# Other homes for the last expert's down weights, and an alternating order of two engines behind the last sort

## The reference

```
y = shared_mlp(x)                                   # silu(x@sg_w) * (x@su_w) @ sd_w, hidden size 1536
for i in range(16):
    gate_feature = x * pe[i] @ gate_w + gate_b
    gate_weight, gate_idx = top_k(gate_feature, 384) # sorted, per token
    u = take(x, gate_idx) * softmax(gate_weight)
    y = y + (silu(u @ eg_w[i]) * (u @ eu_w[i])) @ ed_w[i]
yn = layernorm(y) * ln_g + ln_b
out = x + silu(yn @ m1_w + m1_b) @ m2_w + m2_b
```

## Time and profile before

| | us |
|---|---|
| device time, median of 3 runs | 6455.91 |
| the runs, lowest to highest | 6451.81 to 6457.31 |
| the profiled execution, its own time | 6456.37 |
| its span in the trace | 6454.4 |

### The profile page before, as it was taken

One profiled execution on the slowest core, in us unless ns is written; L12 is line 12 of the kernel. 1 busy time (PEld: TensorE's weight loads), 2 busy tenths in 40 slices (PEclk: granted clock), 3 DMA queues, 4 the chain that ended last, 5 costly groups with the idle time before them and its releaser, 6 DMA issues. The chain is left out here.

```text
span 6454.4 us, 69413 instructions
## 1 busy us (share of the span) xinstructions
PE 5694.2 (88%) x16428; PEld 2987.6 (46%) x16428; DVE 5155.9 (80%) x6434; ACT 2631.7 (41%) x4313; POOL 4120.3 (64%) x3617
## 2 busy tenths in 40 slices
PE   8989999889888888888888888888888888889888
PEld 4545555445444444444444444444444444445554
DVE  4011012999999999999999999999999999999831
ACT  0000000445454545454545454545454545544431
POOL 0543024667777777777777777777777776768630
PEclk9999999999999999999999999999999999999999
DMA  3366245000000000000000000000000000001101
GB/s 124 111 154 163 109 122 156 23 22 15 15 15 16 15 16 15 18 14 30 1 30 1 30 2 29 15 16 15 16 16 15 16 15 16 15 30 37 37 24 45
DMA packets 113766, 254.55 MB, mean 39 GB/s; under 512 B 36104, under 2 KB 46862, under 8 KB 113322
## 3 DMA queue, kind: packets, MB, share of 16 engines
q1 hardware_dynamic: 70442, 180.18, 8.0%
q0 software_dynamic: 42880, 69.46, 4.4%
HBM read 214.75 MB, written 34.58 MB: 39 GB/s over the span
## 5 line engine op out<-in xcount | busy, mean ns | idle before, releaser
L1390 PE MATMUL mask_ps<-key,neg_ident 125*125 125x480 f32 (+7 forms) x4128 | 1886.0, 578 | 477.3 <-DVE key L1787 443.3
L1485 POOL TENSOR_TENSOR pay<-pay_side,pay 125x480 int32<-125x480 int32 (+11 forms) x1075 | 1288.7, 1199 | 643.3 <-DVE pay L1810 637.3
L1669 ACT COPY mask_ps<-key 125x960 f32<-125x960 f32 (+6 forms) x1107 | 947.9, 856 | 1587.4 <-DVE pay L1827 930.6
L1477 POOL TENSOR_TENSOR pay_side<-pay 125x480 int32<-125x480 int32 (+11 forms) x1075 | 1284.6, 1196 | 355.5 <-DVE pay L1827 209.1
L1390 PEld LDWEIGHTS mask_ps<-key,neg_ident 125*125 125x125 f32 x4128 | 732.7, 193 | 1394.7 <-DVE key L1787 882.1
L1810 DVE COPY_PREDICATED pay<-mask_ps,pay 125x960 f32<-125x960 int32 (+6 forms) x1075 | 1231.8, 1146 | 74.4 <-PE mask_ps L1390 54.4
L1777 DVE TENSOR_TENSOR key<-mask_ps,key 125x960 f32<-125x960 f32 (+6 forms) x1075 | 1082.8, 1007 | 20.9 <-PE mask_ps L1390 16.9
L1787 DVE TENSOR_TENSOR key<-mask_ps,key 125x960 f32<-125x960 f32 (+6 forms) x1075 | 1083.9, 1008 | 1.1
L1390 PE MATMUL mask_ps<-key_top,neg_ident 125*125 125x480 f32 (+3 forms) x1472 | 588.3, 527 | 150.8 <-DVE key_top L1787 139.5
L1337 PE MATMUL slot_ps<-w_exp,hid 128*125 128x384 f32 x1920 | 676.1, 491 | 10.4 <-issue 8.7
L1309 PE MATMUL slot_ps<-u_feat,w_exp 128*128 128x312 f32 (+1 forms) x2304 | 666.6, 427 | 0.7 <-ACT u_feat L1564 0.7
(11 more groups left out here) (191 smaller groups left out, 5707.7 us busy)
## 6 DMA issues: line engine op xcount, KB each, us to landing
w_rel_g<-L_gnn_W SPq DMA_DIRECT2D x16, 2304.0 KB, 23.4
w_exp<-L_ffn_ed_w SPq DMA_DIRECT2D x16, 2304.0 KB, 8.4
messages_dram<-rows_g SPq DMA_DIRECT2D x12, 1875.0 KB
w_exp<-L_ffn_eg_w SPq DMA_DIRECT2D x16, 1152.0 KB, 5.4
w_exp<-L_ffn_eu_w SPq DMA_DIRECT2D x16, 1152.0 KB, 7.9
messages_dram<-rows_g SPq DMA_DIRECT2D x20, 375.0 KB
root_w_g<-L_gnn_root SPq DMA_DIRECT2D x2, 2304.0 KB
w_exp<-L_ffn_sg_w SPq DMA_DIRECT2D x4, 1152.0 KB, 5.8
```

The lines of the kernel that those rows point to most:

```text
L1390: last = pe.matmul(mask, neg_ident[0:TP, 0:TP], operand, start=False, stop=True, skip_group_check=True)
L1477: pool.tensor_tensor(shares(pay_was(turn, u), turn, u)[1].bitcast(I32), first, second, ALU.add).then_inc(pays_added, 1)
L1485: pool.tensor_tensor(second, shares(pay_was(turn, u), turn, u)[1].bitcast(I32), first, ALU.subtract).then_inc(pays_taken, 1)
L1669: act.copy(seed_of(turn, u), compared(turn, u)[0]).then_inc(seeded, 1)
```

## The change

Three things are changed, all of them in what follows the last sort.

- The last expert's down weights get places of their own. Four of the six blocks go into `first_rows`, a view of the memory of `h_feat`; they are loaded right behind that expert's gate and up weights. Two blocks go into `w_piece_down`, loaded when the last group of `piece_out` has been filled. A new semaphore `late_loaded` counts the two transfers, and `last_out` takes the place of `expert_out` for this expert on TensorE.
- ScalarE does an exponential and a copy of `piece_out` in turn, five times; then, behind the wait for the inverted sums, a scaling and a copy in turn, five times.
- GpSimd does a `weigh` and a sum of `piece_out` in turn, five times, then the other five sums.

The numbers of operations, of matmuls and of bytes loaded stay the same; one transfer of 2304 KB becomes one of 1536 KB and one of 768 KB.

```diff
--- before.py
+++ after.py
@@ -1042,6 +1042,9 @@
         bias_rows = sb("bias_rows", [TP, D])
         w_exp = sb("w_exp", [P, KD, D])
         w_piece_down = sb("w_piece_down", [P, KK, D])
+
+        NFIRST = KD - 2
+        first_rows = h_feat[:, :, :].rearrange("p k c -> p (k c)")[:, 0:NFIRST * D].rearrange("p (k n) -> p k n", n=D)
         key = sb("key", [TP, NT * D])
         key_top = sb("key_top", [TP, NT * JOINED])
         pay = sb("pay", [TP, NT * D])
@@ -1084,6 +1087,7 @@
         sort_waits, pool_waits = sem("sort_waits"), sem("pool_waits")
         max_ready, exp_ready, inv_ready = sem("max_ready"), sem("exp_ready"), sem("inv_ready")
         weighted, u_ready = sem("weighted"), sem("u_ready")
+        late_loaded = sem("late_loaded")
         block = ctx.enter_context(nc.Block())
 
         def in_banks(view):
@@ -1282,7 +1286,15 @@
             load_piece(2, LAST_BASE + NHALF, LAST_BASE + NHALF)
             load_expert(NEXP - 2, LAST_BASE + NHALF + 2 * SGU, LAST_IN + NIN)
             load_piece(3, CLOSE_BASE, CLOSE_BASE)
-            load_expert(NEXP - 1, CLOSE_BASE + 2 * SGU, END_BASE + NIN)
+            sync.wait_ge(filled, CLOSE_BASE + 2 * SGU)
+            settle(sync, loads_sent)
+            load(w_exp[:, 0:KK, :], by_exp["eg_w"], NEXP - 1, gu_loaded)
+            load(w_exp[:, KK:2 * KK, :], by_exp["eu_w"], NEXP - 1, gu_loaded)
+            sync.dma_start(first_rows, by_exp["ed_w"][NEXP - 1, :, 0:NFIRST, :]).then_inc(late_loaded, 16)
+            sync.wait_ge(filled, END_BASE)
+            settle(sync, loads_sent)
+            sync.dma_start(w_piece_down[:, 0:KD - NFIRST, :], by_exp["ed_w"][NEXP - 1, :, NFIRST:KD, :]).then_inc(
+                late_loaded, 16)
 
         @block.tensor
         def _(pe):
@@ -1331,11 +1343,14 @@
                 if part == 0:
                     if hids is not None:
                         pe.wait_ge(hid_ready, hids + 1)
-                        pe.wait_ge(down_loaded, loads * 16)
+                        if loads is None:
+                            pe.wait_ge(late_loaded, 2 * 16)
+                        else:
+                            pe.wait_ge(down_loaded, loads * 16)
                     room(n)
                 for f in range(part * KK, part * KK + KK):
                     last = pe.matmul(slots[bank][0:TP, 0:HALF], hid[:, f, t * TP:(t + 1) * TP],
-                                     down_w[:, f, half * HALF:(half + 1) * HALF], start=(f == 0), stop=(f == nf - 1))
+                                     down_w(f)[:, half * HALF:(half + 1) * HALF], start=(f == 0), stop=(f == nf - 1))
                 if part == nf // KK - 1:
                     last.then_inc(filled, 1)
 
@@ -1361,7 +1376,12 @@
                                        before(e, 1, 1) + 1)
 
             def expert_out(e, base):
-                return downs(base, KD, w_exp, before(e, 1, 1) + 1, before(e, NGU, SGU) + NGU)
+                return downs(base, KD, lambda f: w_exp[:, f, :], before(e, 1, 1) + 1, before(e, NGU, SGU) + NGU)
+
+            def last_out(e, base):
+
+                return downs(base, KD, lambda f: first_rows[:, f, :] if f < NFIRST else w_piece_down[:, f - NFIRST, :],
+                             None, before(e, NGU, SGU) + NGU)
 
             def piece_in(q, base):
                 return hiddens(base, None, h_feat, KD, KK,
@@ -1369,7 +1389,7 @@
                                before_piece(q, 1, 1) + 1)
 
             def piece_out(q, base):
-                return downs(base + 2 * SGU, KK, w_piece_down, before_piece(q, 1, 1) + 1,
+                return downs(base + 2 * SGU, KK, lambda f: w_piece_down[:, f, :], before_piece(q, 1, 1) + 1,
                              before_piece(q, NGU, SGU) + SGU)
 
             def piece(q, base):
@@ -1417,7 +1437,7 @@
             sort(CLOSING, NEXP, beside(CLOSING, piece_in(3, CLOSE_BASE), 0, 1, CLOSING.n - 3))
             now(piece_out(3, CLOSE_BASE))
             now(expert_in(NEXP - 1, END_BASE))
-            now(expert_out(NEXP - 1, END_BASE + NIN))
+            now(last_out(NEXP - 1, END_BASE + NIN))
 
         @block.gpsimd
         def _(pool):
@@ -1549,9 +1569,11 @@
                                                + piece(LAST_BASE + NHALF), [PAUSE] + expert_in(LAST_IN) + [PAUSE] + expert_out(LAST_IN + NIN), 2))
             sort(CLOSING, NEXP, beside(CLOSING, hiddens(CLOSE_BASE, KD, KK), 2, 1, CLOSING.n - 3))
             features_sorted(CLOSING, NEXP, CLOSING.n)
+            adds = downs(CLOSE_BASE + 2 * SGU, KK)
             for t in range(NT):
                 weigh(NEXP - 1, t)
-            now(downs(CLOSE_BASE + 2 * SGU, KK))
+                now(adds[t:t + 1])
+            now(adds[NT:])
             now(expert_in(END_BASE))
             now(expert_out(END_BASE + NIN))
 
@@ -1749,12 +1771,14 @@
                 [PAUSE] + expert_in(NEXP - 2, LAST_IN) + [PAUSE] + expert_out(NEXP - 2, LAST_IN + NIN), 1), CLOSING)
             sort(CLOSING, NEXP, beside(CLOSING, piece_in(3, CLOSE_BASE), 1, 1, CLOSING.n - 3))
             keys_sorted(CLOSING, NEXP, NEXP - 1, CLOSING.n)
+            sums = piece_out(3, CLOSE_BASE)
             for t in range(NT):
                 exponentials(NEXP - 1, t)
-            now(piece_out(3, CLOSE_BASE))
+                now(sums[t:t + 1])
             act.wait_ge(inv_ready, NEXP)
             for t in range(NT):
                 scale(NEXP - 1, t)
+                now(sums[NT + t:NT + t + 1])
             now(expert_in(NEXP - 1, END_BASE))
             now(expert_out(NEXP - 1, END_BASE + NIN))
```

## The result

| | before | after |
|---|---|---|
| device time, median of 8 runs, us | 6453.77 | 6434.89 |
| the runs, lowest to highest | 6445.94 to 6458.85 | 6433.82 to 6438.11 |
| span of the profiled execution | 6454.4 | 6433.1 |

The ratio is 0.9974, with a 95% interval of 0.9965 to 0.9984: 10 to 23 us less. The forecast was 6438.6, with 6434.5 to 6445.0 as its range; the direction holds, and the median lies just above the range's lower end, 3.7 us under the forecast.

The account below looks back on a forecast made before the run. After the last sort, TensorE's stops and the low clock behind them were taken as the bound. Terms 7.28 + 1.86 + 3.86 + 2.92 + 1.35 = 17.27 us off 6456.37, median 0.46 lower, gave 6438.6 us; range 6434.5 to 6445.0.

Parts of the forecast that it names:

- step 1, the stop for the weights: Ahead of the last expert's down matmuls, TensorE starts at 6289.13 instead of 6296.41: 7.28 us; a 1.4 us stop remains.
- step 1, clock in the down groups: In the last expert's two down products, the clock stays high behind the shorter stop: 1.86 us, bounds 0 and 1.86.
- step 2, restart against `neg_max`: Behind the sort, the first copy follows the first exponential, so TensorE resumes at 6218.84 instead of 6222.70: 3.86 us.
- step 2, clock in the eight groups: In the eight remaining `piece_out` groups, the clock doesn't fall, so they take 15.50 us, not 18.42: 2.92 us.
- step 3, end of `piece_out` to hidden groups: Scalings are done ahead, so `turned` starts 1.60 us after `piece_out` ends on TensorE instead of 2.95: 1.35 us.
- hidden groups: The last expert's hidden groups still start at the low clock after sparse transposes; no change taken, 2.35 us the bound.
- rival 1: The clock falls at the shorter stops too: 6443.4 us if at both, 6440.5 to 6441.5 at one; chance 0.20.
- still 1.00 after 4 us: Argument that the clock would hold through the shortened stops: in the long stops it was still high after 4 us.
- the lag: GpSimd's pairs take 2.14 us against 1.94 per group, yet TensorE is never late, with 0.7 us to spare.
- the table loads: Alternating exponentials and copies on ScalarE adds no table switches; nine loads would give 6448.1 us, chance 0.01.
- Rival 2: The clock holds through the denser transposes before the hidden groups, saving 2.35 us more: 6436.2 us; chance 0.10.
- The slower rival: The clock, low at the hidden groups' start, does not come back over them: up to 37 us, 6476; chance 0.03.

Follow-up runs that it names:

- after_again: The changed kernel once more, unchanged, timed beside the kernel before and profiled a second time: stage 106.87 us, ratio 0.9976.
- e1_weights_only: Against the kernel before, only the last expert's down weights get their new homes; ScalarE and GpSimd keep the old order: stage 114.56 us, ratio 0.9995.
- e4_filler: The whole change plus four useless TensorE matmuls in the stop behind the first two `piece_out` groups: stage 105.28 us, ratio to before 0.9973.
- e3_own_buffer: The whole change, with copies of `piece_out` and the last `expert_out` sent to a separate buffer in `feat`: stage 104.70 us, ratio to before 0.9974.
- the last two kernels: The change with two copies ahead of the exponentials and a separate buffer, without and with useless matmuls among the transposes: stages 99.34 and 99.49 us.

## Why the prediction was right, and where not

| term | forecast | the change | `after_again` |
|---|---|---|---|
| step 1, the stop for the weights | 7.28 | 8.69 - 1.43 = 7.26 | 7.26 |
| step 1, clock in the down groups | 1.86 | 1.66 | 1.66 |
| step 2, restart against `neg_max` | 3.86 | 6.99 - 3.14 = 3.85 | 3.86 |
| step 2, clock in the eight groups | 2.92 | 18.42 - 18.76 = -0.34 | 18.42 - 15.74 = 2.68 |
| step 3, end of `piece_out` to hidden groups | 1.35 | 6.10 - 4.43 = 1.67 | 1.52 |
| hidden groups | 0 | 40.50 - 39.80 = 0.70 | -0.58 |
| sum | 17.27 | 14.80 | 16.40 |

The sums of the terms agree with the stages (14.79 and 16.40 us less) to 0.01 us. Step 1 was right in both terms, shown by `e1_weights_only`. The large weights stand in the new places long before they are used, and the next thing that was late was GpSimd's last `hid`, by the 1.4 us forecast.

Step 2 was right in the first copy. Its other term, "I take it that it doesn't fall now", is the step that failed in the first profile; rival 1 came true there, at one stop of two. One reason was a wrong constant: I took the stop as 5.63 - 3.86 = 1.77 us, from a profile whose first two groups had run slowly. The stop's length is not fixed. It is what is left between the end of these groups and the first copy, 1.8 us after a slow start and 3.3 after a fast one, and in these profiles the clock held through the short one and fell in the long one (`e4_filler` shows that it was the stop). The other reason was the fall itself: "still 1.00 after 4 us" was read from one stop, and in the change the clock fell some 2.6 us into the stop; had it lasted 4 us there as well, the stop of 3.3 us would have done no harm. The forecast described one of two forms as the only one. (Its "0.50 in 6224 to 6228" is not in the earlier trace rows; the row stands above and says so.)

GpSimd's pairs took 2.1 us against 1.94 of a group, as worked out, and the lag never reached TensorE (`e4_filler`); the table loads stayed at two in the stage (6208.50 and 6234.43), none of them between an exponential and a copy. The Trainium skill, "ScalarE: Activation LUTs", "Table sets: the hidden batching unit", asks to batch calls by table set and not by function, and says that cheap functions, copy among them, are in every set. The trace agrees, so this alternation was never what that rule warns of. Step 3 was right: `turned` 0 began at T + 1.62 (forecast 1.60), released by the last sum, and `e3_own_buffer` shows this wait to be the one that ends last. It gained 0.3 us more since from there to the hidden groups it was 2.81 us (6231.65 to 6234.46) and not the 3.15 of before; the mean granted clock over this stretch was 1.00 in the change (6230.0 to 6234.4) and 0.84 before (6241.0 to 6247.2). Rival 2, a clock that holds through the transposes, did not come true in the change (0.50 at the hidden groups' start), only in the last two kernels. The slower rival did not occur: the low stretch of the hidden groups ended within 7 us each time.

The measured difference of the medians, 18.9 us, is more than the 14.8 to 16.4 us found in the stage. The interval of the ratio, 10 to 23 us, holds both, and the second timing of the same two kernels gave medians of 6454.70 and 6439.77, 14.9 us apart. So that the first median lies under the forecast while the stage gained 0.9 to 2.5 us less than forecast is luck, with a graph part that spreads over 11 us; what makes that part vary was not tested.

## What to carry to other kernels

Behind a pipeline's last round, what stands in each engine's list no longer has cover. Look there for work that needs nothing from the last result but is queued behind work that does: the copies of the first two groups were worth 5.2 to 6.8 us more than the alternation when moved ahead. Give a last load its own place when buffers of earlier stages lie idle. And do not price a stop by subtraction from one profile when a slow clock ahead of it may have hidden part of it.

## What the runs showed of the hardware

The granted clock makes one kernel take two forms. The same stretch, first groups to the end of the eight, took 23.0 us after a low clock at the sort's end and 26.1 after a high one: here the faster start gave the slower end. Behind its last work TensorE kept the high clock for some 2.6 us in one stop and 4.2 in another. The clock fell over the transposes or right behind them in most profiles, but it stayed at 1.00 through all of it, 3.7 us with TensorE busy for 2.45, in the first kernel with all ten groups in one piece and the separate buffer. A table load took 1.28 us, and the exponential began 0.01 us after its end. The graph part varied by 11 us between executions of like code, and by 8.5 us between two of the same kernel, more than most of the terms weighed here.
